# An empty place between the first and the second pair of row tiles in the pipeline of the last stage

## What is computed

```python
xn = layernorm(x)
h = xn
for l in range(2):                       # graph attention layers
    h_new = elu(attention over the edges of (h @ Wsrc[l], h @ Wdst[l]))
    h = layer_norm(h_new + h, ln_w[l], ln_b[l])
x = x + layer_norm(h, on_w, on_b) + linear_attention(xn)
x = x + gelu(layernorm(x) @ in_weight.T + in_bias) @ out_weight
```

## Time and profile before

| | |
|---|---|
| median of 3 executions | 2290.95 us (2289.56 to 2295.0) |
| profiled execution, its own time | 2295.07 us |
| its span | 2293.2 us |
| TensorE busy | 2142.6 us, 93% of the span |
| VectorE busy | 1670.7 us, 73% |
| ScalarE busy | 1122.0 us, 49% |
| mean granted TensorE clock | 0.974 |

### The profile page before, as it was taken

One profiled execution on the slowest core, in us unless ns is written; L12 is line 12 of the kernel. 1 busy time (PEld: TensorE's weight loads), 2 busy tenths in 40 slices (PEclk: granted clock), 3 DMA queues, 4 the chain that ended last, 5 costly groups with the idle time before them and its releaser, 6 DMA issues. The chain is left out here.

```text
span 2293.2 us, 91571 instructions
## 1 busy us (share of the span) xinstructions
PE 2142.6 (93%) x32341; PEld 1718.5 (75%) x32342; DVE 1670.7 (73%) x4413; ACT 1122.0 (49%) x2757; POOL 770.8 (34%) x798
## 2 busy tenths in 40 slices
PE   5999998999899999999997899899999999999578
PEld 3665554555799999999996556589999999999457
DVE  5223996344688888888888774488888888888873
ACT  1101210014566666666664324466666666666463
POOL 0000001111455555555553001255555555554000
PEclk9999999999999999999998899999999999999789
DMA  5000223323788888888884024488888888887301
GB/s 189 0 1 8 79 96 87 112 94 96 217 252 250 250 252 251 252 250 250 251 251 155 33 85 120 126 243 251 251 251 251 250 248 251 252 240 241 132 22 47
DMA packets 139237, 397.61 MB, mean 173 GB/s; under 512 B 21705, under 2 KB 76268, under 8 KB 139124
## 3 DMA queue, kind: packets, MB, share of 16 engines
q0 software_dynamic: 59584, 298.64, 43.1%
q1 hardware_dynamic: 76525, 90.41, 12.6%
q10 hardware_dynamic: 3044, 7.45, 1.0%
HBM read 368.18 MB, written 16.78 MB: 168 GB/s over the span
## 5 line engine op out<-in xcount | busy, mean ns | idle before, releaser
L498 ACT ACTIVATE at_relu<-at_turned,ah_attn_size 128x512 f32<-128x512 f32 x1092 | 719.3, 696 | 432.7 <-PE at_turned L557 431.4
L479 POOL DMA_INDIRECT at_rows<-table,ah_index x360 | 360.7, 1002 | 296.0 <-DVE ah_index L681 104.0
L479 POOL DMA_INDIRECT ah_room<-table,ah_index x352 | 351.7, 999 | 292.8 <-DVE ah_index L681 123.4
L555 PE MATMUL at_turned<-ah_place,dst_rows 96*128 96x128 bf16 x2208 | 401.2, 223 | 19.8 <-issue 9.6
L557 PE MATMUL at_turned<-ident,ah_room 128*128 128x128 f32 x2208 | 416.6, 279 | 0.0
L557 PE MATMUL at_turned<-ident,at_rows 128*128 128x128 f32 x2160 | 403.4, 277 | 1.4 <-issue 1.4
L555 PE MATMUL at_turned<-at_place,dst_rows 96*128 96x128 bf16 x2160 | 388.9, 222 | 0.0
L677 DVE SCALAR_TENSOR_TENSOR sums<-sums,at_factor,at_total 128x97 f32 x1456 | 343.8, 309 | 9.1 <-issue 6.0
L557 PEld LDWEIGHTS at_turned<-ident,ah_room 128*128 128x128 f32 x2208 | 317.6, 144 | 24.6
L557 PEld LDWEIGHTS at_turned<-ident,at_rows 128*128 128x128 f32 x2160 | 308.1, 143 | 24.1 <-issue 1.7
L667 DVE TENSOR_TENSOR at_spread<-at_lined,at_weight 128x1024 f32<-128x1024 f32 x182 | 223.0, 1225 | 132.4 <-ACT at_weight L508 119.3
(11 more groups left out here) (318 smaller groups left out, 3198.1 us busy)
## 6 DMA issues: line engine op xcount, KB each, us to landing
at_flags<-run_flags SPq DMA_DIRECT2D x182, 64.0 KB
dst_rows<-pr_parts SPq DMA_DIRECT2D x76, 144.0 KB, 2.6
ah_place<-local_rows SPq DMA_DIRECT2D x92, 96.0 KB
at_place<-local_rows SPq DMA_DIRECT2D x90, 96.0 KB
table<-ah_room SPq DMA_DIRECT2D x20, 400.0 KB, 2.4
ah_room<-table,ah_index POOLq DMA_INDIRECT x368
at_rows<-table,ah_index POOLq DMA_INDIRECT x360
mx_w<-in_L_mix_W_qkv SPq DMA_DIRECT2D x2, 2304.0 KB, 18.8
```

The source lines that it names most:

```text
L479: pool.indirect_dma_start(rows[b][:, j, :], None, table, bass.IndirectOffsetOnAxis(index[b][:, j:j + 1], 0)).then_inc(gathered[b], 16)
L498: act.activation(relu[c][:], turned[chunk(b, c)][:], ACT.Relu, scale=attn_size[:, c:c + 1]).then_inc(bent, 1)
L555: pe.matmul(into, dst_rows[:, bass.ds(at[j], 1), c * P:(c + 1) * P].rearrange("p o d -> p (o d)"), place[b][:, j * P:(j + 1) * P], start=T ...
```

## The change

The list of parts gets an empty part at place 1, so there are six places and ten turns (-2 to 7) in place of nine. The first pair, tiles 0 and 1, keeps its place; each later pair is reached one turn later. What a turn does with an empty part falls away. Around this:

- `tiles` reads the list; `put_behind` names the two tiles whose product VectorE adds in a turn, which for tiles 0 and 1 is the turn in which tiles 2 and 3 come to the feed-forward, as before.
- The number of tiles with a second move buffer is NT - 4 in place of NT - 2, since moves of tiles 6 and 7 now stand between the products of the first pair.
- In the turn of the first feed-forward ScalarE does the activation of tile 0 behind the squares of `Settle` in place of ahead of them, and the activation of tile 1 at the end of the turn after it.
- `scales` leaves empty parts out of the turns' ends; where an empty part lies between two others its two columns are included, and a memset at the stage's start fills them.

```diff
-        dve, here = step.engine, [kind for kind in range(self.kinds) if 0 <= turn - kind < len(self.parts)]
+        dve, here = step.engine, [kind for kind in range(self.kinds) if 0 <= turn - kind < len(self.parts) and self.parts[turn - kind][1]]
...
-LAST_PARTS = tuple((t, 2) for t in range(0, NT, 2))
+LAST_PARTS = ((0, 2), (2, 0), *((t, 2) for t in range(2, NT, 2)))
...
-        y_loaded = ctx.enter_context(signals(nc, [f"fi_y_loaded{g}" for g in range(len(LAST_PARTS))]))
+        y_loaded = ctx.enter_context(signals(nc, [f"fi_y_loaded{g}" for g in range(NT // 2)]))
...
-        settle = Settle(nc, sb, moved_ps, "se", LAYERS - 1, sums, nodes, ident, ln_w, ln_b, norms, out_ps, NT - 2)
+        settle = Settle(nc, sb, moved_ps, "se", LAYERS - 1, sums, nodes, ident, ln_w, ln_b, norms, out_ps, NT - 4)
...
-            return range(2 * part, 2 * part + 2) if 0 <= part < len(LAST_PARTS) else ()
+            return range(LAST_PARTS[part][0], sum(LAST_PARTS[part])) if 0 <= part < len(LAST_PARTS) else ()
+
+        def put_behind(part):
+            return range(LAST_PARTS[part][0] - 2, LAST_PARTS[part][0]) if 0 < part < len(LAST_PARTS) and LAST_PARTS[part][1] else ()
...
-                    for t in out_of[0:1]:
-                        gelu(t)
+                    late = turn == SCALED
+                    if not late:
+                        for t in out_of[0:1]:
+                            gelu(t)
                     for t in tiles(turn - SUMMED):
                         square_y(t)
                     for t in tiles(turn + 1):
                         settle.square(act, t)
+                    if late:
+                        gelu(out_of[0])
                     for t in tiles(turn + 2):
                         settle.bend(act, t)
-                    for t in out_of[1:2]:
-                        gelu(t)
+                    if turn == SCALED + 1:
+                        gelu(1)
+                    if not late:
+                        for t in out_of[1:2]:
+                            gelu(t)
...
-                    if turn < SCALED:
+                    if turn < SCALED or not tiles(turn - SCALED):
                         for t in moving:
                             settle.move(pe, t)
...
+                step(dve.memset(norms.spread[:, SCALED, norms.width:2 * norms.width], 1.0))
...
-                    closing, summing, done = tiles(turn), tiles(turn - SUMMED), tiles(turn - SCALED - 1)
+                    closing, summing, done = tiles(turn), tiles(turn - SUMMED), put_behind(turn - SCALED)
```

More of the change, by code:

```diff
@@ L1887, in _ @@
                 sp.dma_start(bias[:], in_bias.rearrange("(c p) -> p c", p=P), allow_slow_non_contiguous=True).then_inc(w_out_loaded, 16)
-                for g in range(1, len(LAST_PARTS)):
+                for g in range(1, NT // 2):
                     load_y(g)
```

## The result

The change makes the kernel slower by 0.4%. Five executions of the changed kernel have a median of 2301.94 us (2301.8 to 2305.61), five of the kernel before 2292.46 us; the ratio is 1.0044, with a 95% interval of 1.0032 to 1.0056, which is 7.3 to 12.8 us. The forecast was +12.1 us and 2303.0 us.

What follows compares the result with a forecast made beforehand. The last stage was taken as a chain through VectorE, then TensorE alone, with almost no slack behind T2. Terms -9.5 (T), +19.0 (T to T2) and +2.6 (restart) gave +12.1 us on 2290.95: 2303.0 us, range 2296.0 to 2308.5.

Steps and rivals of the forecast that it cites:

- T: Start of the `normalize` of tile 0 in the last stage; forecast to move by -9.5 us, to 2179.2.
- the wait that it laid bare: VectorE's wait for the square of tile 1 ahead of the scale in turn -1: 1.2 us.
- T to T2: From the `normalize` of tile 0 to that of tile 2 (T2): grows from 23.9 to 42.9 us, +19.0.
- The three waits: VectorE's waits ahead of the takes of tiles 6, 7 and 9: 6.8, 3.4 and 2.0 us.
- The move of tile 9 at the low clock: TensorE's move of tile 9 in the empty turn: 2.81 us, or 1.54 if the clock were high.
- The moved activation costs nothing: Activation of tile 0 behind ScalarE's squares: no cost, as the squares run while ScalarE would wait for TensorE.
- The restart: Second feed-forward starts at the low clock after TensorE's rest: 2.6 us lost, bounds 0 to 4.1.
- I take 5.5 us of low clock: Assumed low-clock time at the second feed-forward: turning loses 0.64 us, the other 4.0 us lose 2.0.
- No slack behind T2: A delay of tile 2's `normalize` reaches the end whole, but for 0.89 us that TensorE waits ahead of 2231.81.
- Leaving the clock out: The sum without the low-clock loss at the second feed-forward: 9.5 in place of 12.1 us.
- The rival that the clock stays high: TensorE's clock stays high, wholly or mostly: three clock terms won back, +4.7 to +7 us, 2295.7 to 2298; chance 0.12.
- The rival that the waits vanish: No move waited for; `normalize` of tile 2 follows tile 0's by VectorE's 30.5 us, time 2288.1 at high clock; chance 0.05.

Runs made afterwards that it cites:

- e3_moves_ahead: Changed kernel with the moves of tiles 6 and 7 ahead of the first `turn_node`: stage 147.51 us, ratio 1.0004 to the kernel before.
- e5_own_psum: Changed kernel with tile 9 moved into a PSUM tile of its own, so its move needn't wait for the take of tile 8: stage 155.14 us.
- e7_both: Changed kernel with the moves of tiles 6 and 7 ahead of the first `turn_node` and tile 9 in its own PSUM tile: stage 146.32 us.
- e1_act_order: Changed kernel with ScalarE's order of the kernel before, the empty place kept: stage 156.57 us, ratio 1.0047 to the kernel before.
- e2_late_only: Kernel before, without the empty place, with only the activation of tile 0 put behind the squares: stage 146.22 us, ratio 0.9996.
- e4_warm: Changed kernel with unneeded matmuls added in TensorE's idle times of the empty turn: stage 154.40 us, ratio 1.0032 to the kernel before.
- e9_both_warm: `e7_both` with 92 unneeded matmuls added behind the move of tile 9: stage 143.80 us, ratio 0.9990 to the kernel before.
- e8_before_ahead_warm: Kernel before with moves of tiles 8 and 9 ahead, activation of tile 0 behind the squares, 36 unneeded matmuls before tile 2: stage 143.68 us, ratio 0.9993.

## Why the prediction was right

- **The time.** +12.1 us was forecast; +10.7 us was measured in the stage, 9.5 us between the medians of five. That 2303.0 us lies within 1.1 us of the 2301.94 measured is partly luck: the sum was too long by 1.4 us, and the median of three that it started from (2290.95) was 1.5 us below the later one of five.
- **T.** Forecast -9.5 us, measured -9.73. The work of one pair went behind T; the wait that it laid bare is 1.14 us where 1.2 was said. The places on the time axis, 2179.2 and 2222.1, came 4 us earlier, as the whole stage did in that profile.
- **T to T2.** Forecast 42.9 us, measured 42.77. The three waits were forecast as 6.8, 3.4 and 2.0 us and measured as 6.60, 3.30 and 1.95. `e3_moves_ahead`, `e5_own_psum` and `e7_both` took them away and got back 10.06, 2.67 and 12.10 us. The move of tile 9 at the low clock was read rightly too (2.81 us).
- **The moved activation costs nothing.** `e1_act_order` and `e2_late_only` show it, within 0.6 and 0.3 us.
- **The restart** was the term that was mis-sized: 2.6 us forecast, 1.48 measured. The step that was off is "I take 5.5 us of low clock"; it was 3.1 us. The prediction's own working, with 3.1 us put in, gives 0.64 + 0.8 = 1.4 us, so the mechanism holds. `e4_warm` gives the same cost (1.46) from the other side, and the other kernels 1.4 to 2.8 us, so the term is not a constant of the kernel: in `e7_both` the 5.5 us would have been right. The forecast's own bounds, 0 to 4.1 us, held it.
- **No slack behind T2.** Right: in `e4_warm` T2 comes 17.6 us later behind T than before the change, with the clock high, and the turn behind it still takes 18.22 us; from the `normalize` of tile 4 to the end the kernels before and after differ by 0.01 us.
- **Leaving the clock out** would have given +9.5 in place of +12.1; the measured +10.67 lies between, so here it was as near as my count. The Trainium skill (TensorE: Matmul & The Clock Gate, Part 1: The HAM clock gate) allows this for a model of a whole kernel, where it puts the ramp at under 1% of the span; the trace agrees, since the 2.73 us that `e4_warm` got back are 0.1% of 2300 us. Of a change of 10.7 us they are a quarter. That sum wasn't free of the clock either: it kept the 1.27 us that the move of tile 9 loses by it.
- **The rival that the clock stays high** is out, by the falls at 2167.3, ahead of T, and at 2201.4 in the changed kernel. **The rival that the waits vanish** is out for this change, and `e7_both` shows that its price was right: T to T2 of 30.67 us against 30.5 in the prediction. The price in time, 2.8 us less than before if the clock is high, is met by `e9_both_warm` with 2.7 us in the stage; with the low clock of `e7_both` only 0.2 us are left.

The sum of the stage, +10.67 us, agrees with the times of executions: 0.44% of 2292.46 is 10.1 us.

## What to carry to other kernels

An empty place in a pipeline moves work from ahead of an event to behind it, and what decides is which waits the moved work had been covering. Look, for each wait on the busy engine, at what stands ahead of it in its stream and whether that leaves. Count also what an extra turn adds by itself (here a scale and a wait, 3.5 us of VectorE) and which engine sets the event: here the extra work was free only against a kernel in which ScalarE set it. And reckon with the clock: in the five forms with the empty place and nothing to keep TensorE busy in it, the first work behind it ran at the low clock, at a cost of 1.4 to 2.8 us.

## What the runs showed of the hardware that I had not expected

The moment at which the clock comes back after a rest ranged from 2.8 us (`e1_act_order`) to 5.6 us (`e7_both`) behind the first matmul of uninterrupted work at the same place of the program, which is worth 1.4 us.

The moment at which it falls varies as much. Behind the last transpose of the weight it fell after 1.4 us of rest in `e1_act_order`, 1.9 in the changed kernel and 2.3 before the change; behind the move of tile 8, after 2.5 us in the changed kernel and 5.4 in `e1_act_order`, where TensorE had done the same work. The 2.3 us ahead of the `turn_node` of tile 2 before the change brought no fall. Rows of the changed kernel for its 1.9 us, TensorE's last work ahead of T and the slice of the fall:

```profile
2164.50 0.88 PE L2004 MATMUL fi_turned<-ident,fi_w_in_rows 128*128 128x128 f32 x6 [0.90 <-ACT fi_w_in L1935]
...
2167.00:2168.00 1.00, 0.00 (x0) 0.00 (x0) 0.93 (x5) 0.91 (x3) 0.00 (x0) 0.64 0.00 0
```

It can also fall amid work. In the five forms with the moves ahead, TensorE rests for 1.0 to 2.8 us ahead of each `turn_node` of the first pair, and the clock fell once there: in four of them 0.3 to 0.6 us into a `turn_node`, and in `e8_before_ahead_warm` just ahead of the second. Rows of `e7_both`, where the second of these takes 1.27 us and the slice from 2436 to 2437 us reads 0.75, a fall at 2436.5:

```profile
2434.35 0.88 PE L1982 MATMUL fi_turned<-ident,nodes 128*128 128x128 f32 x6 [1.47 <-ACT nodes L1922]
2436.22 1.27 PE L1982 MATMUL fi_turned<-ident,nodes 128*128 128x128 f32 x6 [0.99 <-ACT fi_node_t L1928]
```

The chips differ by 11% on this kernel. The kernel before took 2292 to 2293 us on the first, 2547 us on the second and 2549 us on the third, and none of it is in the last stage. Of the page of `e8_before_ahead_warm`, on the second chip, the slices' bandwidth and the gathers of rows by index:

```profile
GB/s 170 1 1 65 13 146 113 79 108 183 211 210 207 210 212 210 209 210 214 208 210 103 28 121 93 181 209 213 211 200 217 208 201 215 212 213 207 171 14 49
...
L479 POOL DMA_INDIRECT ah_room<-table,ah_index x352 | 405.9, 1153 | 372.6 <-DVE ah_index L681 190.9
```

In the profile before, on the first chip, the slices in which the second chip stays near 210 GB/s read about 250, and one such instruction took 999 ns in place of 1153. `e9_both_warm` on the third chip reads like the second. Why these two move 210 GB/s is not settled by any run here.
